# Second attention of a fused transformer block: turned weights in two 64-row tiles, values and projections in every second step

## The chip, the core and the metric

The kernel runs on one core of one Trainium2 chip, as one launch. Its time is device microseconds (us) from start to end, the median of three runs: 1046.44 us (1045.92 to 1047.82). The core has a matrix engine (TensorE, PE in the profile, with its weight loads shown apart as PEld), VectorE (DVE), ScalarE (ACT), GpSimd (POOL), and SyncE (SP), which issues DMAs. PSUM is what PE writes its results to, in eight banks.

## The reference

Six residual parts follow each other on x, 8 sequences of 256 tokens by 128 channels, in float32. The change touches only the fifth:

```
x = x + 0.5 * _L0_ffn_ref(_layernorm(x), ...)      # stage f0
x = x + _L0_attn_ref(_layernorm(x), ...)           # a0
x = x + 0.5 * _L0_ffn_ref(_layernorm(x), ...)      # g0
x = x + 0.5 * _L1_ffn_ref(_layernorm(x), ...)      # f1
x = x + _L1_attn_ref(_layernorm(x), ...)           # a1: what is changed
x = x + 0.5 * _L1_ffn_ref(_layernorm(x), ...)      # g1

def _attn_forward(X, Wq, bq, Wk, Wv, Wproj, bproj, Wr, br, b_nd):   # 16 heads of 64
    Q = X @ Wq + bq;  K = X @ Wk;  V = X @ Wv
    R = X @ Wr + br                                # 10 numbers a head and token
    extra = einsum('bhtn,ntp->bhtp', R, D_ntT)     # a learned bias by distance
    logits = Q @ K^T / 8 + causal mask + extra
    A = softmax(logits) @ V
    return A @ Wproj + bproj
```

## The kernel before, in words

Stage a1 is `attention_one`. It goes through 8 batches of 8 steps: 64 steps n, each for one pair of heads of one batch b, with u = n mod 8 the step within the batch. Every engine has its own program, in order; semaphores tie them.

For a pair (two heads, 256 queries by 256 keys; the causal half is left out, so 3 blocks of 128x128 a head):

- `scores` (PE, L2655): Q times K^T into PSUM banks 0 and 1, one head each, from the 64 rows 0 to 63 and the 64 rows 64 to 127 of the array. A float32 product is two instructions in the profile, so x8.
- `logits` (DVE, L2839 and L2841): adds the bias and takes the row's least value. Two heads a step. `scores` of the next step waits for both (`l_ready`).
- `probabilities` (ACT, L2781 and L2783): exp and row sums, two heads.
- `invert` and `normalise` (DVE, L2849, L2585, L2586): divides by the sums.
- `turn` (PE, L2667): in step n for pair n - 1, six 128x128 transposes, head i into bank 2 + i. It waits for the normalised weights (`pn_ready`) and for the bank (`pT_ready`).
- `take_turned` (ACT, L2791): two copies of 128x384, PSUM to PT.
- `values` (PE, L2687): in step n for pair n - 3, weights times V into bank 4, each head in its own 64 columns of the array.
- `take_values` (ACT, L2799): a 128x256 copy of bank 4 to AT (the profile calls it a_xn).
- `project` (PE, L2700, once a batch at u = 3): A times Wproj, 32 instructions, then `add` on DVE (L2858).

Between these PE makes pieces for a later batch, each one PSUM bank: Q, K, V and R projections in three parts of reduced precision (L743 to L745), and G, the bias tables, by `tables` (L2611, two 40-row matmuls side by side a pair of pieces). STEPS and `pair_pieces` say which step makes which piece: before, one Q in every even step and its K in the next odd step, V in steps u = 5, 6, 7, R at u = 0, and a G pair at u = 1 to 4. `pieces_stored` copies them out of PSUM, odd numbers mostly by ACT, even ones by DVE, after the step's logits (DVE) or exps (ACT). Three banks are used in turn for pieces.

Within a step PE's order is: scores, tables, values, projections, (project), turn. DVE's is: logits, pieces, invert and normalise. ACT's is: take_turned of pair n - 2, exps, pieces, take_values.

Of the kernel before, what the change touches and what calls it, by code (L numbers as in the profile page):

```python
# [19 lines left out]
ACT = mybir.ActivationFunctionType  # L20
# [3 lines left out]
P = 128  # L24
BATCH = 8
# [2368 lines left out]
def attention_one(core, name, ctx, w):  # L2394
# [26 lines left out]
    def chunk(b, c):  # L2421
# [4 lines left out]
    SLOTS = 4  # L2426

    VLAG = 3
    TSLOTS = 2 * VLAG
    L = sb("L", [P, SLOTS, 3 * P])  # L2430
    least = sb("least", [P, SLOTS, 2])
# [25 lines left out]

    STEPS = ([("R", 0), ("QK", 0)], [("G", 0), ("G", 1), ("QK", 1)], [("G", 2), ("G", 3), ("QK", 2)],  # L2460
             [("G", 4), ("G", 5), ("QK", 3)], [("G", 6), ("G", 7), ("QK", 4)],
             [("QK", 5), ("V", 0)], [("QK", 6), ("V", 1), ("V", 2)], [("QK", 7), ("V", 3)])
# [4 lines left out]
    def pair_pieces(n):  # L2467

        found = []
        for b in range(2, BATCH, 2):  # L2470
            for j in range(CH):
                first = CH * b + 2 * j - QK_AHEAD
                for which, at in (("Q", first), ("K", first + (j < CH - 1))):
                    if at == n:
                        found.append((b, (which, j)))
        return found

    def in_step(n):

        b, u = n // CH, n % CH  # L2480
        own = [(b + 1, k) for k in STEPS[u] if k[0] != "QK" or b == 0] if b + 1 < BATCH else []
        return ([k for k in own if k[1][0] in "RG"] + pair_pieces(n) + [k for k in own if k[1][0] not in "RG"]
                + ([(b - 1, ("O", 0))] if u == VLAG and b else []))
# [104 lines left out]
    def tensor(pe):  # L2588
# [68 lines left out]
                        last.then_inc(s_done, 1)  # L2657

        def turn(b, c):
            for i in range(2):  # L2660
                n = b * H1 + 2 * c + i
                pe.wait_ge(pn_ready, n + 1)
                if n >= 2:

                    pe.wait_ge(pT_ready, n - 1)
                for j in range(3):
                    last = pe.transpose(bank[2 + i][:, P * j:P * j + P], pr[:, n % SLOTS, P * j:P * j + P],  # L2667
                                        core.ident[:, :])
                last.then_inc(p_turned, 1)

        def values(b, c):
            s, m = b % 2, b * CH + c
            pe.wait_ge(pT_ready, 2 * m + 2)
            if c == 0:
                for j in range(4):
                    wait_piece(pe, b, "V", j)
            if m:

                pe.wait_ge(aT_ready, m)
# [3 lines left out]
            o = bank[4]  # L2683
            for kt, keys, queries in ((0, slice(0, SEQ), slice(0, SEQ)), (1, slice(SEQ, 3 * P), slice(P, SEQ))):
                for i in range(2):
                    h = 2 * c + i
                    last = pe.matmul(o[D1 * i:D1 * i + D1, queries], V[s][:, kt, D1 * h:D1 * h + D1],  # L2687
                                     PT[:, (2 * m + i) % TSLOTS, keys], start=(kt == 0), stop=(kt == 1),
                                     skip_group_check=True)
            last.then_inc(pv_done, 1)  # L2690

        def project(b):

            pe.wait_ge(aT_ready, CH * (b + 1))
# [14 lines left out]
        for n in range(BATCH * CH + VLAG):  # L2709
            b, u = n // CH, n % CH  # L2710
            if b < BATCH:
                scores(b, u)
            if b + 1 < BATCH:
                tables(n)
            if 0 <= n - VLAG:
                values((n - VLAG) // CH, (n - VLAG) % CH)
            if b < BATCH:
                projections(n)
            if u == VLAG and b:
# [50 lines left out]
    def scalar(act):  # L2770
        act.wait_ge(core.const_ready, 4)
        act.activation(ln.unused[:, 0:1], core.ones[:, 0:1], ACT.Exp)
        ln.take_quarter(act, 0)

        def probabilities(n):
            o = n % SLOTS
            act.wait_ge(l_ready, n + 1)
            if n >= SLOTS:

                act.wait_ge(p_turned, n - SLOTS + 1)  # L2780
# [5 lines left out]
        def take_turned(n):  # L2786
            act.wait_ge(p_turned, n + 1)
            if n >= TSLOTS:

                act.wait_ge(pv_done, (n - TSLOTS) // 2 + 1)  # L2790
            act.activation(PT[:, n % TSLOTS, :], bank[2 + n % 2][:, 0:3 * P], ACT.Copy).then_inc(pT_ready, 1)  # L2791

        def take_values(m):
            b, c = m // CH, m % CH
            act.wait_ge(pv_done, m + 1)
            if b:

                act.wait_ge(piece_done, at(b - 1, ("O", 0))[0] + 1)
            act.activation(AT[:, c, :], bank[4][:, 0:SEQ], ACT.Copy).then_inc(aT_ready, 1)  # L2799

        for n, k in enumerate(FIRST):
            if by_act(k):
                store_piece(act, True, 0, k)
            if n in (6, 10, 14):
                ln.take_quarter(act, (6, 10, 14).index(n) + 1)
        for n in range(BATCH * CH + VLAG):
            b, u = n // CH, n % CH
            if 2 <= n < BATCH * CH + 2:
                for i in range(2):
                    take_turned(2 * (n - 2) + i)  # L2810
# [5 lines left out]
            if 0 <= n - VLAG:  # L2816
                take_values(n - VLAG)

    def vector(dve):
        ln.statistics_of(dve, 0, 4)  # L2820
# [42 lines left out]
                store_piece(dve, False, 0, k)  # L2863
        for n in range(BATCH * CH):
            b, u = n // CH, n % CH
            if u == VLAG + 1 and b:
                add(b - 1)
            for i in range(2):
                logits(b, 2 * u + i)
# [144 lines left out]
```

## Time and profile before

| | us |
|---|---|
| median of three runs | 1046.44 |
| profiled execution, span from first to last instruction | 1041.4 |
| stage a1, first scores to the last add | 615.72 to 904.10 |
| PE, DVE, ACT busy over the span | 893.2, 759.6, 524.4 |

The profiled execution's span is 5.0 us less than the median time; what lies outside the span is not in the trace. In a list of instructions the first number is the start in us from the span's start, the second how long the group took. Matmuls overlap: one may start while the one before still drains, so the distance between starts tells what a matmul costs, not its own duration.

### The profile page before, as it was taken

The page shows a single profiled execution, that of the slowest core. Times are in us where ns is not written, and L with a number is a line of the kernel's source. Part 1 is how long each engine was busy: PE and PEld are TensorE (multiplying, and loading weights), DVE is VectorE, ACT ScalarE, POOL GpSimd, SP SyncE. Part 2 cuts the span into 40 slices and gives each one's busy share as a digit, 9 for nine tenths or more (in the row PEclk, how much of TensorE's full clock was granted, in tenths as well). Part 3 has the DMA queues.
Part 4 walks back from the last instruction along what each step waited for, and adds up shares of the span by engine and source line. Part 5 has one row for each costly group of instructions (what it writes and reads, how often), then busy time and mean ns, then how long its engine had stood idle before and what let it go on. Part 6 is the DMA issues. An engine that isn't in the chain of part 4 may idle for free.

```text
span 1041.4 us, 22929 instructions
## 1 busy us (share of the span) xinstructions
PE 893.2 (86%) x7108; PEld 676.9 (65%) x7108; DVE 759.6 (73%) x2654; ACT 524.4 (50%) x1461; POOL 287.2 (28%) x395
## 2 busy tenths in 40 slices
PE   5899979999996899945999199999999999649992
PEld 4467756666765357834999167777777776437992
DVE  7758888787767866877676757787678777566675
ACT  4232044555564323023455258787778778534553
POOL 3034046543001003127755260001000000067751
PEclk9999996998997999965999589999999999958997
DMA  9204089800005204065320266435634642153413
GB/s 233 69 2 137 1 312 374 257 5 1 3 1 159 77 1 138 1 189 164 90 73 29 81 205 201 142 105 160 197 101 130 182 143 61 58 166 84 109 35 125
DMA packets 134948, 119.73 MB, mean 115 GB/s; under 512 B 10755, under 2 KB 115227, under 8 KB 134836
## 3 DMA queue, kind: packets, MB, share of 16 engines
q1 hardware_dynamic: 130292, 109.83, 35.5%
q0 software_dynamic: 4544, 8.54, 2.5%
q8 instruction: 55, 0.90, 0.4%
q14 instruction: 57, 0.47, 0.1%
HBM read 67.45 MB, written 51.80 MB: 115 GB/s over the span
## 4 chain that ended last, share of the span: by engine, by line
PE 75%; DVE 14%; issue 4%; ACT 3%; DMA 2%; DVEq 1%; SPq 0%; POOL 0%; POOLq 0%; ACTq 0%
PE psum L955 7%; PE psum L964 7%; PE psum L1551 6%; PE psum L1465 4%; PE psum L2655 4%; PE psum L2687 4%; PE psum L743 3%; PE psum L2667 3%; PE psum L2139 3%; PE psum L2611 3%; PE psum L2700 3%; PE psum L2077 3%; PE psum L745 2%; PE psum L744 2%; PE psum L2042 2%
## 5 line engine op out<-in xcount | busy, mean ns | idle before, releaser
L2297 DVE TENSOR_REDUCE a_negmax<-psum 128x2 f32<-128x512 f32 x128 | 83.9, 684 | 24.2 <-PE psum L2077 22.8
L2246 ACT ACTIVATE a_PT<-psum 128x1024 f32<-128x1024 f32 x64 | 65.5, 1023 | 28.0 <-PE psum L2122 27.6
L2781 ACT ACTIVATE a_pr<-a_L,a_least 128x128 f32<-128x128 f32 x128 | 50.8, 397 | 38.5 <-DVE a_least L2841 38.1
L2687 PEld LDWEIGHTS psum<-a_PT,a_V 128*64 128x64 f32 x512 | 32.8, 136 | 47.6 <-issue 24.1
L2783 ACT ACTIVATE a_pr<-a_L,a_least 128x256 f32<-128x256 f32 x128 | 63.6, 497 | 0.0
L1010 ACT ACTIVATE f_hT<-psum,f_wt 128x128 f32<-128x128 f32 x156 | 44.5, 369 | 36.2 <-PE psum L955 36.2
L2687 PE MATMUL psum<-a_PT,a_V 128*64 128x256 f32 (+1 forms) x512 | 55.7, 337 | 7.0 <-ACT a_xn L2799 6.9
L1010 ACT ACTIVATE g_hT<-psum,g_wt 128x128 f32<-128x128 f32 x156 | 44.5, 369 | 33.5 <-PE psum L955 33.5
L2655 PE MATMUL psum<-a_KT,a_Q 64*128 64x128 f32 (+1 forms) x512 | 59.3, 350 | 0.3 <-DVE a_least L2841 0.3
L2791 ACT ACTIVATE a_PT<-psum 128x384 f32<-128x384 f32 x128 | 55.4, 488 | 0.7 <-PE psum L2667 0.6
L2116 PE MATMUL psum<-a_turned 24*128 24x256 f32 x256 | 55.4, 366 | 0.0
L2841 DVE CUSTOM_DVE_ANT_0 a_L<-psum,a_X 128x256 f32<-128x256 f32 x128 | 53.7, 419 | 0.0
L2077 PE MATMUL psum<-a_turned 24*128 24x256 f32 x224 | 52.5, 346 | 0.9 <-ACT a_turned L2212 0.7
L2667 PE MATMUL psum<-ident,a_pr 128*128 128x128 f32 x384 | 52.8, 274 | 0.0
L163 POOL MEMSET g_logit<- 128x128 f32 x1 | 0.2, 205 | 180.4 <-DVEq L2916 180.4
L2667 PEld LDWEIGHTS psum<-ident,a_pr 128*128 128x128 f32 x384 | 44.9, 141 | 7.5 <-issue 1.4
L2122 PE MATMUL psum<-a_shift,ahead_select 32*128 32x256 bf16 x256 | 48.4, 294 | 0.0
L896 POOL DMA_INDIRECT f_back_dram<-f_y,f_xin x39 | 41.3, 1059 | 25.6 <-DVE f_y L1093 22.0
L896 POOL DMA_INDIRECT g_back_dram<-g_y,g_xin x39 | 40.9, 1048 | 25.0 <-DVE g_y L1093 21.3
L2839 DVE CUSTOM_DVE_ANT_0 a_L<-psum,a_X 128x128 f32<-128x128 f32 x128 | 36.7, 286 | 14.6 <-PE psum L2655 14.3
L955 PE MATMUL psum<-f_xT,f_wt 128*128 128x128 f32 x312 | 43.2, 284 | 3.1 <-DVE f_xT L1087 3.1
L2586 DVE TENSOR_SCALAR a_pr<-a_pr,a_rinv 128x256 f32<-128x256 f32 x128 | 45.5, 355 | 0.0
(579 smaller groups left out, 2593.7 us busy)
## 6 DMA issues: line engine op xcount, KB each, us to landing
z<-a_G SPq DMA_DIRECT2D x32, 512.0 KB, 3.4
a_X<-z SPq DMA_DIRECT2D x16, 1024.0 KB, 6.8
f_slots_dram<-empty SPq DMA_DIRECT2D x1, 8910.0 KB, 28.1
g_slots_dram<-empty SPq DMA_DIRECT2D x1, 8910.0 KB, 51.3
a_X<-z SPq DMA_DIRECT2D x16, 512.0 KB, 4.0
f_wgu<-in_gate_up SPq DMA_DIRECT2D x16, 384.0 KB, 6.9
z<-pad SPq DMA_DIRECT2D x6, 1024.0 KB, 9.8
g_wgu<-in_gate_up SPq DMA_DIRECT2D x16, 384.0 KB, 6.3
```

Of the source, the lines that this page charges most:

```text
L896: pool.indirect_dma_start(back_dram[:, :], bass.IndirectOffsetOnAxis(ap=xin[:, i, P:P + 1].bitcast(I32), axis=0), y[i % YBUF][:, :], None, ...
L955: last = pe.matmul(bank[i % 2][:, P * c:P * c + P], wt[i % WBUF][:, P * c:P * c + P], xT[:, i % 2, :], start=True, stop=True)
L964: last = pe.matmul(bank[4 + i % 2][:, 0:P], hT[:, i % 2, c, :], wt[i % WBUF][:, OUT + P * c:OUT + P * c + P], start=(c == 0), stop=(c == F ...
L1010: act.activation(hT[:, i % 2, c, :], bank[i % 2][:, P * c:P * c + P], ACT.Relu, bias=wt[i % WBUF][:, B1 + c:B1 + c + 1]).then_inc(relu_don ...
L1551: last = pe.matmul(sum_bank[g], ypart[:, p, i, :].bitcast(F32R), ST[:, p % RING, BLOCK * g:BLOCK * g + BLOCK].bitcast(F32R), start=(p == 0 ...
L2077: last = pe.matmul(bank[h % 2][:, SEQ * t:SEQ * t + SEQ], q[rows, g, P * t:P * t + P].bitcast(F32R), k[rows, g, :].bitcast(F32R), start=Tr ...
L2246: act.activation(PT[m % 4][:, :, :, :].rearrange("p j t n -> p j (t n)"), core.psum[:, 2 + 2 * (u % 2):4 + 2 * (u % 2), :], ACT.Exp, scale ...
L2297: dve.tensor_reduce(negmax[:, :, h], query_bank(b, h).rearrange("p (t n) -> p t n", n=SEQ), AX.X, ALU.max, negate=True).then_inc(max_done, 1)
L2655: last = pe.matmul(out, Q[rows, at, b % 2, queries], KT[rows, at, b % 2, keys], start=True, stop=True)
L2667: last = pe.transpose(bank[2 + i][:, P * j:P * j + P], pr[:, n % SLOTS, P * j:P * j + P], core.ident[:, :])
L2687: last = pe.matmul(o[D1 * i:D1 * i + D1, queries], V[s][:, kt, D1 * h:D1 * h + D1], PT[:, (2 * m + i) % TSLOTS, keys], start=(kt == 0), st ...
L2783: act.activation(pr[:, o, P:3 * P], L[:, o, P:3 * P], ACT.Exp, bias=least[:, o, 1:2], scale=-1.0, accum_out=sums[:, o, 1:2]).then_inc(p_re ...
```

## The change

1. `turn` splits every 128x128 transpose into two, from rows 0 to 63 and rows 64 to 127 of the weights: 12 transposes of 64 rows, each moving 64 columns. Rows 0 to 63 of both heads go to bank 2, rows 64 to 127 to bank 3. It waits once for the copy of the whole pair before (`pT_ready`, m).
2. `take_turned` is one ACT copy for a pair, 768 elements a partition out of two banks.
3. `values` runs only in even steps, for pairs n - 4 and n - 3, into the two halves of bank 4. `take_values` is one 128x512 copy for both.
4. All Q, K, V and R pieces are made in even steps; G pairs in odd steps (but for one in step 2 of the first batch). R and the first G pair of a batch are made two batches ahead, at u = 6 and 7. `project` moves from u = 3 to u = 4.

```diff
+    STEPS = ([("QK", 0), ("QK", 1)], [("G", 2), ("G", 3)], [("QK", 2), ("QK", 3), ("V", 0)], [("G", 4), ("G", 5)],
+             [("QK", 4), ("QK", 5), ("V", 1)], [("G", 6), ("G", 7)], [("QK", 6), ("QK", 7), ("V", 2), ("V", 3)], [])
+    SECOND = {0: [("R", 0)], 1: [("G", 0), ("G", 1)], 2: [("G", 2), ("G", 3)]}
+    FIRST_GATES = {6: [("R", 0)], 7: [("G", 0), ("G", 1)]}
...
-                first = CH * b + 2 * j - QK_AHEAD
-                for which, at in (("Q", first), ("K", first + (j < CH - 1))):
-                    if at == n:
-                        found.append((b, (which, j)))
+                if CH * b + 2 * j - QK_AHEAD == n:
+                    found += [(b, ("Q", j)), (b, ("K", j))]
...
         def turn(b, c):
+            m = b * CH + c
+            if m:
+                pe.wait_ge(pT_ready, m)
             for i in range(2):
...
-                if n >= 2:
-                    pe.wait_ge(pT_ready, n - 1)
                 for j in range(3):
-                    last = pe.transpose(bank[2 + i][:, P * j:P * j + P], pr[:, n % SLOTS, P * j:P * j + P],
-                                        core.ident[:, :])
-                last.then_inc(p_turned, 1)
+                    for r in range(2):
+                        rows = slice(HP * r, HP * r + HP)
+                        at = HP * (3 * i + j)
+                        last = pe.transpose(bank[2 + r][:, at:at + HP], pr[rows, n % SLOTS, P * j:P * j + P],
+                                            core.ident[rows, rows])
+            last.then_inc(p_turned, 1)
...
-            if 0 <= n - VLAG:
-                values((n - VLAG) // CH, (n - VLAG) % CH)
+            if n % 2 == 0 and n >= VSTEP:
+                for m in (n - VSTEP, n - VLAG):
+                    values(m // CH, m % CH)
...
-            act.activation(PT[:, n % TSLOTS, :], bank[2 + n % 2][:, 0:3 * P], ACT.Copy).then_inc(pT_ready, 1)
+            own = PT[:, 2 * (m % VLAG):2 * (m % VLAG) + 2, :].rearrange("p i n -> p (i n)")
+            act.activation(own.rearrange("p (k r c) -> p r k c", r=2, c=HP),
+                           core.psum[:, 2:4, 0:3 * P].rearrange("p r (k c) -> p r k c", c=HP),
+                           ACT.Copy).then_inc(pT_ready, 1)
...
-            act.activation(AT[:, c, :], bank[4][:, 0:SEQ], ACT.Copy).then_inc(aT_ready, 1)
+            act.activation(AT[:, c:c + 2, :].rearrange("p c n -> p (c n)"), bank[4], ACT.Copy).then_inc(aT_ready, 1)
```

How PE's order changes in the steady part of the stage. Before, one whole step (u = 1 of a later batch); L2655 is scores, L2611 tables, L2687 values, L743 to L745 the K piece, L2667 turn:

```order
L2655 MATMUL psum<-a_KT,a_Q 128x128 x2
L2655 MATMUL psum<-a_KT,a_Q 128x256 x2
L2611 MATMUL psum<-early_bnd,a_RT 128x512 x2
L2687 MATMUL psum<-a_PT,a_V 64x256 x2
L2687 MATMUL psum<-a_PT,a_V 64x128 x2
L743 MATMUL psum<-a_xs_high,early_wk_rest 128x512
L744 MATMUL psum<-a_xs_rest,early_wk_high 128x512
L745 MATMUL psum<-a_xs_high,early_wk_high 128x512
L2667 MATMUL psum<-ident,a_pr 128x128 x6
```

Now, from a K piece at the end of the even step u = 0 through the odd step u = 1; L2683 is turn, L2667 scores, L2623 tables:

```order
L743 MATMUL psum<-a_xs_high,early_wk_rest 128x512
L744 MATMUL psum<-a_xs_rest,early_wk_high 128x512
L745 MATMUL psum<-a_xs_high,early_wk_high 128x512
L2683 MATMUL psum<-ident,a_pr 128x64 x12
L2667 MATMUL psum<-a_KT,a_Q 128x128 x2
L2667 MATMUL psum<-a_KT,a_Q 128x256 x2
L2623 MATMUL psum<-early_bnd,a_RT 128x512 x2
L2683 MATMUL psum<-ident,a_pr 128x64 x12
```

Values and the K piece have left the odd step; what stays in it, and the turn before it, use 64 or 40 rows of the array and all 128 columns.

ACT, before, at the end of such a step (exps, pieces, values copy, the two turned copies, the next exps):

```order
L2781 ACTIVATE a_pr,a_sums<-a_L,a_least 128x128
L2783 ACTIVATE a_pr,a_sums<-a_L,a_least 128x256
L2731 ACTIVATE a_G<-psum 128x512
L2731 ACTIVATE a_KT<-psum 128x512
L2799 ACTIVATE a_xn<-psum 128x256
L2791 ACTIVATE a_PT<-psum 128x384 x2
```

Now, at the end of the even step u = 0:

```order
L2798 ACTIVATE a_pr,a_sums<-a_L,a_least 128x128
L2800 ACTIVATE a_pr,a_sums<-a_L,a_least 128x256
L2748 ACTIVATE a_KT<-psum 128x512
L2819 ACTIVATE a_xn<-psum 128x512
L2809 ACTIVATE a_PT<-psum 128x2x6x64
```

The G piece has moved to the odd step, the values copy is twice as wide and comes every second step, and the turned copy is one instruction, still behind all of these.

## Rows read from the trace of the kernel before

**Rows 1.** The page: busy time of the engines

```profile
PE 893.2 (86%) x7108; PEld 676.9 (65%) x7108; DVE 759.6 (73%) x2654; ACT 524.4 (50%) x1461; POOL 287.2 (28%) x395
```

**Rows 2.** Stretches: from:to, length, busy of engines; batches 0, 1-5, 6, 7

```profile
615.72:649.39 33.67, 31.91 (x236) 22.46 (x235) 27.78 (x130) 26.73 (x97) 2.26 (x5) 1.00 0.70 205
649.39:830.96 181.57, 181.09 (x1331) 129.78 (x1330) 137.94 (x623) 140.52 (x491) 5.38 (x8) 1.00 0.50 146
830.96:865.79 34.83, 34.83 (x261) 24.87 (x260) 26.43 (x123) 27.00 (x96) 0.00 (x0) 1.00 0.51 152
865.79:904.10 38.31, 31.14 (x271) 23.40 (x270) 22.49 (x119) 28.52 (x102) 0.00 (x0) 1.00 0.01 2
```

**Rows 3.** PE instructions in order of time: start, took, instruction

```profile
790.79 0.93 PE L2655 MATMUL psum<-a_KT,a_Q 64*128 64x128 f32 x8
791.65 0.87 PE L2687 MATMUL psum<-a_PT,a_V 128*64 128x256 f32 x8
792.45 0.50 PE L743 MATMUL psum<-a_xs_high,early_wk_rest 128*128 128x512 f32 x1
792.79 0.39 PE L744 MATMUL psum<-a_xs_rest,early_wk_high 128*128 128x512 f32 x1
793.02 0.40 PE L745 MATMUL psum<-a_xs_high,early_wk_high 128*128 128x512 f32 x1
...
797.89 0.82 PE L2667 MATMUL psum<-ident,a_pr 128*128 128x128 f32 x6
798.64 0.93 PE L2655 MATMUL psum<-a_KT,a_Q 64*128 64x128 f32 x8
799.39 1.03 PE L2611 MATMUL psum<-early_bnd,a_RT 40*128 40x512 f32 x4
```

**Rows 4.** The chain, same columns: a G pair and a project

```profile
843.96 0.86 PE psum L2611 x4
846.51 3.57 PE psum L2700 x32
```

**Rows 5.** PE instructions elsewhere, at half clock (last row: that stretch's clock)

```profile
332.00 1.81 PE L1393 MATMUL psum<-g_wr,g_xnT 128*128 128x64 f32 x8
333.60 1.06 PE L632 MATMUL psum<-ident,g_xn 128*128 128x128 f32 x4
334.45 3.52 PE L1393 MATMUL psum<-g_wr,g_xnT 128*128 128x64 f32 x16
...
329.40:337.90 8.50, 8.50 (x43) 8.50 (x43) 7.98 (x40) 5.26 (x11) 0.00 (x0) 0.50 1.05 291
```

**Rows 6.** Step 40: its scores, and the first and last row of its logits

```profile
794.69 0.93 PE L2655 MATMUL psum<-a_KT,a_Q 64*128 64x128 f32 x8
...
795.64 0.29 DVE L2839 CUSTOM_DVE_ANT_0 a_L<-psum,a_X 128x128 f32<-128x128 f32 x1 [0.15 <-PE psum L2655]
796.76 0.08 DVE L2841 DVE_READ_ACCUMULATOR2_ANT a_least<- 128x1 f32 x1
```

**Rows 7.** DVE and ACT in the last batch, where PE is not full

```profile
885.99 0.28 DVE L2839 CUSTOM_DVE_ANT_0 a_L<-psum,a_X 128x128 f32<-128x128 f32 x1
886.66 0.40 ACT L2781 ACTIVATE a_pr<-a_L,a_least 128x128 f32<-128x128 f32 x1 [0.35 <-DVE a_least L2841]
888.43 0.36 ACT L2799 ACTIVATE a_xn<-psum 128x256 f32<-128x256 f32 x1
889.22 0.28 DVE L2839 CUSTOM_DVE_ANT_0 a_L<-psum,a_X 128x128 f32<-128x128 f32 x1
```

**Rows 8.** ACT groups by shape: mean ns of one after the busy time

```profile
L2791 ACT ACTIVATE a_PT<-psum 128x384 f32<-128x384 f32 x80 | 34.6, 489 | 0.0
L2731 ACT ACTIVATE a_G<-psum 128x512 f32<-128x512 f32 x20 | 11.6, 580 | 0.0
L2246 ACT ACTIVATE a_PT<-psum 128x1024 f32<-128x1024 f32 x64 | 65.5, 1023 | 28.0 <-PE psum L2122 27.6
```

**Rows 9.** DVE group: a G piece copied out of PSUM

```profile
L2744 DVE COPY a_G<-psum 128x512 f32<-128x512 f32 x20 | 13.7, 686 | 0.0
```

More of the change, by code:

```diff
@@ L2428, in attention_one @@
     VLAG = 3
+    VSTEP = 4
+    HP = P // 2
     TSLOTS = 2 * VLAG
@@ L2471, in pair_pieces, with gates_in_step @@
             for j in range(CH):
-                first = CH * b + 2 * j - QK_AHEAD
-                for which, at in (("Q", first), ("K", first + (j < CH - 1))):
-                    if at == n:
-                        found.append((b, (which, j)))
-        return found
+                if CH * b + 2 * j - QK_AHEAD == n:
+                    found += [(b, ("Q", j)), (b, ("K", j))]
+        return found
+    def gates_in_step(n):
+        b, u = n // CH, n % CH
+        own = []
+        if b == 0:
+            own += [(1, k) for k in SECOND.get(u, [])]
+        if b + 1 < BATCH:
+            own += [(b + 1, k) for k in STEPS[u] if k[0] == "G" and not (b == 0 and u == 1)]
+        if b + 2 < BATCH:
+            own += [(b + 2, k) for k in FIRST_GATES.get(u, [])]
+        return own
     def in_step(n):
         b, u = n // CH, n % CH
-        own = [(b + 1, k) for k in STEPS[u] if k[0] != "QK" or b == 0] if b + 1 < BATCH else []
-        return ([k for k in own if k[1][0] in "RG"] + pair_pieces(n) + [k for k in own if k[1][0] not in "RG"]
-                + ([(b - 1, ("O", 0))] if u == VLAG and b else []))
+        own = [(b + 1, k) for k in STEPS[u] if k[0] == "V" or (k[0] == "QK" and b == 0)] if b + 1 < BATCH else []
+        return gates_in_step(n) + pair_pieces(n) + own + ([(b - 1, ("O", 0))] if u == VSTEP and b else [])
     pieces, in_bank = {}, [0] * len(PIECE_BANKS)
@@ L2676, in values @@
                     wait_piece(pe, b, "V", j)
-            if m:
-                pe.wait_ge(aT_ready, m)
+            if m >= 2:
+                pe.wait_ge(aT_ready, m // 2)
             else:
@@ L2682, in values @@
                 pe.wait_ge(piece_read[i], first_reads[i])
-            o = bank[4]
+            o = bank[4][:, SEQ * (m % 2):SEQ * (m % 2) + SEQ]
             for kt, keys, queries in ((0, slice(0, SEQ), slice(0, SEQ)), (1, slice(SEQ, 3 * P), slice(P, SEQ))):
@@ L2692, in project @@
         def project(b):
-            pe.wait_ge(aT_ready, CH * (b + 1))
+            pe.wait_ge(aT_ready, CH // 2 * (b + 1))
             _, i, used = at(b, ("O", 0))
@@ L2712, in tensor @@
                 scores(b, u)
-            if b + 1 < BATCH:
+            if b < BATCH:
                 tables(n)
-            if 0 <= n - VLAG:
-                values((n - VLAG) // CH, (n - VLAG) % CH)
+            if n % 2 == 0 and n >= VSTEP:
+                for m in (n - VSTEP, n - VLAG):
+                    values(m // CH, m % CH)
             if b < BATCH:
                 projections(n)
-            if u == VLAG and b:
+            if u == VSTEP and b < BATCH and b:
                 project(b - 1)
@@ L2778, in probabilities @@
             if n >= SLOTS:
-                act.wait_ge(p_turned, n - SLOTS + 1)
+                act.wait_ge(p_turned, (n - SLOTS) // 2 + 1)
             act.activation(pr[:, o, 0:P], L[:, o, 0:P], ACT.Exp, bias=least[:, o, 0:1], scale=-1.0,
@@ L2808, in scalar @@
             if 2 <= n < BATCH * CH + 2:
-                for i in range(2):
-                    take_turned(2 * (n - 2) + i)
+                take_turned(n - 2)
             if b < BATCH:
@@ L2815, in scalar @@
                 pieces_stored(act, True, n)
-            if 0 <= n - VLAG:
-                take_values(n - VLAG)
+            if n % 2 == 0 and n >= VSTEP:
+                take_values(n - VSTEP)
     def vector(dve):
@@ L2865, in vector @@
             b, u = n // CH, n % CH
-            if u == VLAG + 1 and b:
+            if u == VSTEP + 1 and b:
                 add(b - 1)
```

17 lines of the change are left out of this document (7 added, 10 removed).

## The prediction

> **What bounds the kernel now.** I read the page first: PE is busy 86% of the span, DVE 73%, ACT 50% [rows 1]. The reader is to see from it only which engine to follow; what the change is worth is decided in stage a1. So I cut that stage by its batches in the view by windows. In batches 1 to 5 PE is busy 181.09 of 181.57 us, that is 36.31 us a batch without a gap, while DVE and ACT are busy 137.94 and 140.52, some 76%. Batch 6 is full too (34.83 of 34.83). In batch 7, which makes no pieces, PE is busy 31.14 of 38.31 [rows 2]. PE binds 56 steps of 64; the last 8 hang on something else, which the order of time shows: from one pair's logits to the next are 889.22 - 885.99 = 3.23 us, logits, exps, inversion and logits again. The change leaves that loop alone [rows 7].
>
> A PE that is "busy" is not at work all the time, and here the view in order of time matters most. A float32 matmul column costs 0.86 / 1024 = 0.84 ns: a G pair is two instructions of 512 columns on either of two row groups, together 0.86 us [rows 4]. Scores, values and transposes all stream 768 such columns a step (scores and values side by side in two tiles), 0.65 us each. The starts say more than that: transposes to scores 0.75, scores to tables 0.75, scores to values 0.86, values to the K piece 0.80, and in that piece 0.34 to the second part against 0.23 to the third [rows 3]. The surplus sits only where the shape that the array is used in changes (128 rows, 64 rows, 64 columns): transposes to scores 0.10 before and 0.10 after, scores to values 0.11, values to pieces 0.15 on both sides of the values, and 0.11 in the piece's first part. No surplus lies between scores (64 rows) and tables (40 rows). That is 0.57 us for the three changes of shape that each step has.
>
> Check: a batch of before is 8 x (3 x 0.65 + 0.57) = 20.2, 4 Q and 4 K pieces at 3 x 0.23 = 0.69, so 5.5, four V 2.8, R 0.7 (its columns are those of a Q piece), four G pairs 3.4, project 3.57 [rows 4]: 36.1, measured 36.31. The 0.2 is short waits, and I add it to the new sum too.
>
> **The change part by part.**
> Order of work on PE: even steps keep three changes of shape (scores to values to pieces to turn); odd steps are scores, tables, turn, all of 64 or 40 rows, and have none. In the 28 step pairs of batches 0 to 6 that is 28 x 0.57 = 16.0 us less on PE. All else on PE keeps its amount; the second `values` of a pair follows the first in the same shape.
>
> Transposes: 12 of 64 columns in two row groups, for 6 of 128. Where the granted clock was 0.50 (1.2 GHz) the trace has both sizes with 128x128 float32 weights: transposes of 128 columns start (334.45 - 333.60) / 4 = 0.21 us apart, and matmuls of only 64 columns (333.60 - 332.00) / 8 = 0.20 apart [rows 5]. Half the columns bought nothing; the weights, 128 columns in both, set the pace. In `turn` the weights stay 128 columns wide, so each row group needs 0.65 us for its six, as now. The two groups should overlap, as they do for scores, whose eight instructions take the time of four [rows 3]. Bounds: 0.32 us a step if only moved columns counted, 1.29 if the groups did not overlap; I take 0.65, no gain, since that is what both nearest rows give.
> The Trainium skill has rules on both sides. TensorEngine Tiling (Array Packing), section Theoretical Speedup, gives a contraction of at most 64 up to twice the speed; TensorE: Matmul & The Clock Gate, section LDWEIGHTS, says a load costs by its columns and not by its rows. By the first a turn would take 0.32 us, by the second 0.65; the rows at 1.2 GHz agree with the second.
>
> ACT: one 768-wide copy for two of 384 (489 ns each). Between 512 (580) and 1024 (1023) a straight line gives 0.80 us, about 0.70 before the next may start, against two overlapped ones at about 0.8 [rows 8]; bounds 0.49 (one of them alone) and 1.02. Values copy: one of 0.58 [rows 8] for two of 0.36 [rows 7]. ACT gets some 0.2 us a pair of steps back, which nobody waits for.
>
> What is late next: an odd step now holds 0.65 + 0.86 + 0.65 = 2.16 us of PE work, less than others need.
> (a) The next scores wait for both heads' logits. Scores to logits start is 0.95, logits last 1.20 [rows 6]; with 0.1 to hand over, 2.25: at least 0.1 is lost in each odd step.
> (b) Pair u = 0, 1, from the scores of step 0: these waited for the logits of the step before, so its exps (0.89 a head, from (888.43 - 886.66) / 2 [rows 7]) end at 1.3, DVE's inversion of head 1 (0.65) at 2.0, logits of step 0 at 3.2, its exps at 4.5, ACT's K copy (0.5) at 5.0, values copy at 5.5, the turned copy only then, at 6.3. Turn in step 1 waits for it; behind turn stand the scores of step 2, at 6.96. PE's own sum is 4.54 + 2.16 = 6.70.
> (c) Pair 2, 3: DVE's order puts the V piece before the inversion. PE hands V over at 4.5; copy (686 ns long, 0.6 until the next [rows 9]), two inversions and two logits (0.6 + 1.3 + 1.2) end at 7.7; scores at 7.76, PE's sum 5.23 + 2.16 = 7.39.
> (d) Pair 4, 5: 8.80 with V and project, then 2.25: 11.05 for 10.96. Project holds ACT's values copy too, but the turned copy fits in the odd step.
> (e) Pair 6, 7: 6.61 with R and two V, 0.15 for a bank that V waits for, 2.25: 9.0 for 8.77.
> Sum 34.8 for a PE sum of 33.8, so 1.0 of 2.3 us is handed back; with the 0.2 of waits 35.0 against 36.31, 1.3 less a batch.
>
> Over the stage: batches 1 to 5, 5 x 1.3 = 6.5. Batch 0 makes R and the first G pair of batch 2 on top, 0.69 + 0.86, which eats its own 1.5: 0. Batch 6 has given its R and G pair away and its last pair is without Q, K: 2 x 6.96 + 7.76 + 11.05 = 32.8, + 0.2, against 34.83: 1.8. Batch 7 is the 3.23 us loop: an even step there has 3.2 us of PE work, hidden by it. The tail's copy is 0.2 longer (0.58 for 0.36), as the last two pairs' values share it: +0.2. SP's transfers of bias tables start up to one step later for heads 8 to 15 and are needed about seven steps on, and the 35.0 us batch still covers them; the cost if not would be a wait of DVE, none now.
> Total: -6.5 - 1.8 + 0.2 = -8.1. The span of the profiled execution falls from 1041.4 to 1033.3; the median of before, 1046.44, is 5.0 above that span, so 1038.3 us.
>
> **Rivals.**
> A, the forecast: -8.1. Its own range is -13 to -4, from 0.15 us more or less in each of 28 odd steps.
> B, slower: the row groups' transposes do not overlap. Every turn costs 0.64 more. For it: no row here shows a transpose in a half of the rows. Against it: scores and G pairs do overlap, in float32. Price: 56 x 0.64 = 36 on a bound PE, less the 16.0 saved; the odd steps then have no slack to hand back: +20, 1066. It turns slower once a turn costs over 0.15 us more than now.
> C, transposes faster: only moved columns count, 0.32 saved. Odd steps cannot use it, even ones do: 28 x 0.32 = 9 more, 1029. The same time nearly results if the odd steps hand nothing back (-16, 1030). Against C: rows 5.
> D, the odd steps hand all back: each needs 0.6 us more than PE's 2.16, not 0.25. For it: DVE and ACT need 3.23 us a pair by themselves [rows 7], 6.46 in two, and a piece or two on top, near the 6.70 of PE; a copy out of two banks that is slower than a line through the widths of rows 8 adds in (b) straight to the path. Against it: most pieces fit in DVE's wait for exps. Time: 1046, -2 to +2.
> Beside them, the clock after the stage: a stage that ends 8 us earlier meets the changes of the granted clock in the stage behind it at other points of the work; at 1.2 GHz a transpose takes 0.21 us for 0.11 [rows 5, 3], an estimated 2 us either way.
>
> **How the numbers follow.** A 0.62, C 0.15, D 0.13, B 0.10. About 2 us, 0.2%, is what a measurement tells from no change. Faster takes A, C and a quarter of D: 0.80. Same takes half of D: 0.07. Slower: B and the last quarter of D: 0.13. The range 1030 to 1045 holds A, half of C and of D.
>
> **What would show it.** PE's rows after: twelve transposes that start two and two together, 0.107 us from two to two (B: one by one; C: 0.053). No surplus between an odd step's scores, tables and turn. Odd steps of 2.25 to 2.5 us from scores to scores; PE idle before scores (on DVE's logits) and before turn (on ACT's turned copy), together 1 us a batch. A turned copy of 0.8 us. Batches 1 to 5 at 35.0 us, batch 7 at 38. I am wrong if a turn takes other than 0.65 to 0.75, or if odd steps are over 2.7 us, or if the surplus at a change of shape grows where values come in twos.

## The result, and the profile after

The changed kernel takes 1029.77 us (median of 4 runs, 1024.85 to 1031.29); the kernel before, run beside it, 1046.18. The ratio is 0.9857, 95% interval 0.9819 to 0.9895: 15.0 us faster by the ratio (16.4 between the medians), where 8.1 was forecast. The sign and the stage were right, the size was short by nearly half, and 1029.77 lies 0.2 us below the range. A second set of runs of the same kernel gave 1031.15 and a ratio of 0.9864 (0.9824 to 0.9904). Two of the twelve runs of experiment 2 below, its profiled one among them, fell in a slower state of the chip, so its time and ratio are of the other ten.

The page and the view by windows of the changed kernel, to be read against [rows 1, 2]. The windows run from the first scores of a batch to those of the next; columns: from:to, length, then busy time and instructions of PE, PEld, DVE, ACT and POOL, granted clock (1 is full), share of the DMA engines, GB/s.

```profile
span 1028.6 us, 23449 instructions
PE 869.1 (84%) x7492; PEld 662.6 (64%) x7492; DVE 760.1 (74%) x2654; ACT 518.8 (50%) x1365; POOL 286.6 (28%) x395
```

```profile
616.71:650.32 33.61, 29.80 (x280) 21.82 (x279) 28.52 (x127) 25.83 (x84) 3.76 (x6) 1.00 0.64 187
650.32:821.70 171.38, 164.85 (x1571) 120.62 (x1571) 138.06 (x626) 137.67 (x431) 3.87 (x6) 1.00 0.52 153
821.70:853.71 32.01, 30.02 (x299) 21.91 (x299) 25.55 (x122) 26.65 (x86) 0.00 (x0) 1.00 0.49 145
853.71:891.24 37.53, 30.06 (x338) 22.42 (x334) 22.66 (x120) 27.64 (x87) 0.00 (x0) 0.95 0.14 42
```

The reader is to see three things. Batch 0 stayed at 33.6 us, batches 1 to 5 went from 181.57 to 171.38, batch 6 from 34.83 to 32.01, batch 7 from 38.31 to 37.53. Together the stage is 13.8 us shorter, from 288.4 to 274.5 (from the first scores to the last add). The stage starts 1.0 later, what lies behind it is the same 137.4, and 1041.4 - 13.8 + 1.0 = 1028.6, the span. Second, PE is no longer full: 164.85 busy of 171.38, 6.5 us idle where 0.5 was. Third, DVE does what it did (138.06 for 137.94), and ACT 2.9 us less (137.67 for 140.52).

The medians differ by 2 to 4 us more than the two spans, and that is scatter from outside the stage. Each run's time is 1.7 to 1.9 us above its own span, so most of the 5.0 between span and median of before came of a profiled execution that was quicker than the median. In the traces of all kernels here the stage, behind the same code, starts between 611.3 us (mean granted clock so far 0.90, experiment 3) and 620.8 us (0.88, both orders of experiment 5).

PE in order of time, from a K piece through a whole odd step (start, us, instruction), to be held against [rows 3]:

```profile
791.17 0.40 PE L745 MATMUL psum<-a_xs_high,early_wk_high 128*128 128x512 f32 x1
791.49 0.59 PE L2683 MATMUL psum<-ident,a_pr 64*128 64x64 f32 x12
791.92 0.87 PE L2667 MATMUL psum<-a_KT,a_Q 64*128 64x128 f32 x8
792.63 1.02 PE L2623 MATMUL psum<-early_bnd,a_RT 40*128 40x512 f32 x4
793.73 0.59 PE L2683 MATMUL psum<-ident,a_pr 64*128 64x64 f32 x12
```

From the turn's start at 791.49 to the scores' start are 0.43 us, against 0.75 before. The single starts in the trace are two and two together (2 to 4 ns), the second pair 0.11 behind the first and the others 0.061 to 0.064 from pair to pair; before, six starts were 0.109 apart. So 0.32 us went here: 0.10 of a change of shape, and 0.22 of the transposes themselves. That 0.10 is not saved behind a K piece: it now lies ahead of the turn (0.32 from the piece's last part, where 0.23 lies inside a piece). Scores to tables are 0.71, tables to turn 0.86 where PE did not wait (799.95 to 800.82 further on). The turn at 793.73 waited for ACT's copy:

```profile
791.93 0.57 ACT L2748 ACTIVATE a_KT<-psum 128x512 f32<-128x512 f32 x1
792.41 0.57 ACT L2819 ACTIVATE a_xn<-psum 128x512 f32<-128x512 f32 x1
792.89 0.79 ACT L2809 ACTIVATE a_PT<-psum 128x768 f32<-128x768 f32 x1
```

The largest waits of PE and of its weight loads for another engine in batches 1 to 5 (engine, what, waited for: us in total, times, longest). PEld runs ahead of PE, so what it waits is not all lost to PE:

```profile
PEld psum L2683 <- ACT a_PT L2809: 10.5, 20, 0.9
PE psum L2667 <- DVE a_least L2860: 6.2, 11, 0.8
```

The eight steps of batch 5, from scores to scores: before 3.95 4.06 4.07 7.63 4.08 3.90 4.70 3.90 (36.3); after 4.32 2.31 5.02 2.94 8.59 2.26 6.41 2.25 (34.1). The even steps are what PE's starts add up to without a wait. For an odd step they add up to 0.71 + 0.86 + 0.43 = 2.00; what is above 2.00 is waiting, 1.76 us in this batch.

### The profile page after: what moved, and what is told of

Same layout as the page of the kernel before. It is cut to its first block, busy times and chain, and to the rows that moved or that the text cites. A ratio compares the mean times of both kernels' runs of the same rounds, so it can differ in the third digit from the quotient of the medians.

```text
span 1028.6 us, 23449 instructions
## 1 busy us (share of the span) xinstructions
PE 869.1 (84%) x7492; PEld 662.6 (64%) x7492; DVE 760.1 (74%) x2654; ACT 518.8 (50%) x1365; POOL 286.6 (28%) x395
## 4 chain that ended last, share of the span: by engine, by line
PE 65%; DVE 20%; ACT 6%; issue 6%; DMA 2%; DVEq 1%; SPq 0%; POOL 0%; ACTq 0%; POOLq 0%
PE psum L955 7%; PE psum L964 7%; PE psum L1551 6%; PE psum L1465 5%; PE psum L2139 3%; PE psum L2703 3%; PE psum L2716 3%; PE psum L2077 3%; PE psum L2667 2%; PE psum L743 2%; DVE a_negmax L2297 2%; PE psum L1491 2%; PE psum L2042 2%; ACT a_pr L2800 2%; PE psum L745 2%
## 5 line engine op out<-in xcount | busy, mean ns | idle before, releaser
L2667 PE MATMUL psum<-a_KT,a_Q 64*128 64x128 f32 (+1 forms) x512 | 58.5, 346 | 11.1 <-DVE a_least L2860 10.3
L1010 ACT ACTIVATE g_hT<-psum,g_wt 128x128 f32<-128x128 f32 x156 | 44.3, 368 | 33.6 <-PE psum L955 33.6
L2683 PEld LDWEIGHTS psum<-ident,a_pr 64*128 64x128 f32 x768 | 30.6, 139 | 34.6 <-ACT a_PT L2809 21.5
L2809 ACT ACTIVATE a_PT<-psum 128x768 f32<-128x768 f32 x64 | 51.1, 798 | 1.2 <-PE psum L2683 1.2
L2703 PE MATMUL psum<-a_PT,a_V 128*64 128x256 f32 (+1 forms) x512 | 49.5, 335 | 0.1
L955 PE MATMUL psum<-g_xT,g_wt 128*128 128x128 f32 x312 | 42.7, 281 | 2.2 <-DVE g_xT L1087 2.2
L2667 PEld LDWEIGHTS psum<-a_KT,a_Q 64*128 64x128 f32 x512 | 35.1, 190 | 14.1 <-issue 13.8
```

The costliest lines, as they stand in the source:

```text
L955: last = pe.matmul(bank[i % 2][:, P * c:P * c + P], wt[i % WBUF][:, P * c:P * c + P], xT[:, i % 2, :], start=True, stop=True)
L1010: act.activation(hT[:, i % 2, c, :], bank[i % 2][:, P * c:P * c + P], ACT.Relu, bias=wt[i % WBUF][:, B1 + c:B1 + c + 1]).then_inc(relu_don ...
L2667: last = pe.matmul(out, Q[rows, at, b % 2, queries], KT[rows, at, b % 2, keys], start=True, stop=True)
```

## The experiments

The measure that tells kernels apart below is the length of batches 1 to 5 in a profiled execution: the change itself gave 171.38 and, unchanged in a later set, 171.46, while whole times scatter by several us.

**1. The order alone.** The new order, with the turns and their copy as one instruction of 128 rows and contiguous columns.

```diff
                 for j in range(3):
-                    for r in range(2): ...
+                    last = pe.transpose(bank[2 + i][:, P * j:P * j + P], pr[:, n % SLOTS, P * j:P * j + P],
+                                        core.ident[:, :])
```

> The new order of pieces and values, but turn as six 128x128 transposes again (one ACT copy a pair stays). Theory S (a change of the array's shape costs 0.15 to 0.2 us, and a tiled turn 0.43 us against 0.65): the odd step gets two changes back (tables to turn, turn to scores), so a pair of steps has 5 changes, where the changed kernel has 3 and the kernel before 6. PE's odd step is 0.65 + 0.86 + 0.65 + 0.4 = 2.56 us, over the 2.25 that scores and logits need, so it binds again: pairs 0.2 us shorter than before, some 5 us in all, 1040 to 1043. Rival O (the gain is the order itself, values in twos and fewer waits, whatever the shape of turn): 1030 to 1034.

Measured: 1039.77, ratio 0.9966 (0.9942 to 0.9989).

```profile
646.80:824.87 178.07, 177.15 (x1331) 129.65 (x1331) 138.99 (x626) 139.59 (x432) 3.87 (x6) 1.00 0.49 145
```

3.5 us less than 181.57, with PE nearly full (177.15 of 178.07), and a time just under the 1040 to 1043 expected. A turn of 128 rows keeps a change of shape ahead of and behind it, so a pair of steps has five changes for six. The one that goes is values to pieces, 0.25 us in [rows 3] (0.80 for 0.65 behind the values, 0.34 for 0.23 in the piece), 5 us in 20 pairs. Not all of it stays: an odd step needs 2.46 us by PE's starts, and took 2.52 to 2.91.

**2. The tiles alone.** The order of before; `turn`, its wait and its copy as changed.

```diff
+            m = b * CH + c
+            if m:
+                pe.wait_ge(pT_ready, m)
...
-                    last = pe.transpose(bank[2 + i][:, P * j:P * j + P], pr[:, n % SLOTS, P * j:P * j + P], ...
+                    for r in range(2): ...
```

> The order of before, with turn in tiles and one ACT copy a pair. Theory S: three changes of shape a step as before, turn 0.43 for 0.65: 0.2 us in each of 56 steps that PE fills, 11 us less, 1033 to 1037. Rival (tiles are worth nothing but for the change of shape they save, my forecast's 0.65 for a turn): 1044 to 1047.

Measured: 1040.54, ratio 0.9959 (0.9926 to 0.9993), where 1033 to 1037 was expected.

```profile
652.49:830.39 177.90, 171.62 (x1576) 116.56 (x1574) 137.09 (x624) 138.43 (x451) 5.45 (x9) 1.00 0.51 150
```

```profile
798.24 0.39 PE L745 MATMUL psum<-a_xs_high,early_wq_high 128*128 128x512 f32 x1
798.57 0.59 PE L2671 MATMUL psum<-ident,a_pr 64*128 64x64 f32 x12
798.99 0.87 PE L2656 MATMUL psum<-a_KT,a_Q 64*128 64x128 f32 x8
```

The turn takes 0.42 here too, so its saving belongs to the tiles and not to the order. The change of shape has moved from behind the turn to ahead of it (piece to turn 0.33, against 0.23 inside a piece): still six a pair. A step without a wait is 0.28 shorter (u = 1: 3.78 for 4.06), so 40 steps were to give 11 us. 3.7 went, and PE is idle 6.3 us, most of it before `values`, which wait for ACT's copy of bank 4:

```profile
PE psum L2691 <- ACT a_xn L2805: 5.1, 10, 0.7
```

Order alone -3.5, tiles alone -3.7, both -10.2. Both together take the changes of shape out of the odd step, which neither does alone, and the new order has half as many copies of bank 4 to wait for; no run parts these two.

**3. Twelve plain products.** `turn` as changed, in float32 matmuls with the identity instead of transposes.

```diff
-                        last = pe.transpose(bank[2 + r][:, at:at + HP], pr[rows, n % SLOTS, P * j:P * j + P],
-                                            core.ident[rows, rows])
+                        last = pe.matmul(bank[2 + r][:, at:at + HP], pr[rows, n % SLOTS, P * j:P * j + P],
+                                         core.ident[rows, rows], start=True, stop=True)
```

> The changed kernel with the same twelve tiles turned as plain float32 products with the identity instead of transposes: two instructions each, same weights of 64x128, same 64 moved columns. Theory W (a float32 product's weight load of 128 columns takes 0.107 us and sets the pace, a transpose's takes half): 12 pairs of starts 0.107 apart, turn 1.29 us, time 1055 to 1066. Rival M (moved columns set the pace in both): 0.054 to 0.063 apart, turn 0.65 to 0.75, time 1034 to 1040.

Measured: 1060.08 (one run), within the 1055 to 1066 of theory W.

```profile
647.89:845.02 197.13, 197.13 (x2054) 158.15 (x2054) 139.33 (x626) 142.84 (x432) 3.86 (x6) 1.00 0.45 134
```

```profile
801.35 1.55 PE L2683 MATMUL psum<-ident,a_pr 64*128 64x64 f32 x24
802.74 0.88 PE L2667 MATMUL psum<-a_KT,a_Q 64*128 64x128 f32 x8
```

The same shapes (weights of 64 x 128, 64 moved columns), but 24 instructions for 12, and the pairs 0.112 apart instead of 0.062: turn to scores 1.39 us, against 0.43. The products of `project`, which move 128 columns, are 0.112 apart as well (3.57 / 32 [rows 4]), so for products half the moved columns buy nothing, as I had read from [rows 5]. The weight loads differ in the same sense. PEld by line and shape: count, busy us, mean ns of one, idle before. First the changed kernel, then this one:

```profile
L2667 PEld LDWEIGHTS psum<-a_KT,a_Q 64*128 64x128 f32 x321 | 21.9, 188 | 8.7 <-issue 8.6
L2703 PEld LDWEIGHTS psum<-a_PT,a_V 128*64 128x64 f32 x320 | 19.8, 137 | 12.4 <-issue 6.6
L2683 PEld LDWEIGHTS psum<-ident,a_pr 64*128 64x128 f32 x480 | 19.1, 138 | 19.2 <-ACT a_PT L2809 10.5 <-issue 8.0
```

```profile
L2683 PEld LDWEIGHTS psum<-ident,a_pr 64*128 64x128 f32 x912 | 55.4, 188 | 14.7 <-issue 9.6 <-ACT a_PT L2809 4.5
```

A load of 128 columns lasts 188 ns for a product and 138 for a transpose, as long as a product's load of 64 columns (137). That the loads set the pace in both cases is argued from this and not shown. The trace of before had this sign, and the prediction did not use it (the same view, turn and scores):

```profile
L2667 PEld LDWEIGHTS psum<-ident,a_pr 128*128 128x128 f32 x242 | 28.8, 141 | 4.8
L2655 PEld LDWEIGHTS psum<-a_KT,a_Q 64*128 64x128 f32 x322 | 21.1, 186 | 6.8 <-issue 6.5 <-ACT a_Q L2755 0.2 <-DVE x L2858 0.2
```

**4. Values apart.** The second `values` of a pair behind the pieces, on the same work. What was expected counts two more changes of shape in each even step. It is one: pieces to values and values to turn are new, but pieces to turn is gone. Only at u = 4, where `project` stands between values and turn, are there two.

```diff
-                for m in (n - VSTEP, n - VLAG):
-                    values(m // CH, m % CH)
+                values((n - VSTEP) // CH, (n - VSTEP) % CH)
             if b < BATCH:
                 projections(n)
+            if n % 2 == 0 and n >= VSTEP:
+                values((n - VLAG) // CH, (n - VLAG) % CH)
```

> The changed kernel, but the second values of an even step stand behind the projections: no work more or less, two more changes of shape in each of 28 even steps. Theory S: 0.15 to 0.2 us for the first (pieces to values) and the same for the second (values to turn, as values to pieces before): 0.35 x 28 = 10 us more than the changed kernel, 1038 to 1042. Rival (the surplus at a change of shape is a wait on data that would be elsewhere without it): 1029 to 1033.

Measured: 1034.71, ratio 0.9914 (0.9883 to 0.9945).

```profile
652.80:826.73 173.93, 170.83 (x1570) 119.38 (x1571) 138.76 (x626) 138.81 (x431) 3.73 (x6) 1.00 0.51 152
```

```profile
794.87 0.40 PE L745 MATMUL psum<-a_xs_high,early_wk_high 128*128 128x512 f32 x1
795.20 0.87 PE L2703 MATMUL psum<-a_PT,a_V 128*64 128x256 f32 x8
796.00 0.58 PE L2683 MATMUL psum<-ident,a_pr 64*128 64x64 f32 x12
```

The steps by themselves give the price: u = 0 went from 4.32 to 4.47 and u = 2 from 5.02 to 5.17, 0.15 for one change, without a wait in either; u = 4 went from 8.59 to 8.94, 0.35 for two. At u = 6 (6.41 to 7.18) only 0.15 of the 0.77 is shape. The rest is in the last two pieces, both V: PE now reaches them before their banks are free. In batch 5 they start 0.31 and 0.57 us behind the part before, where 0.23 is usual, and each begins at the slow pace of a first part. The second of them:

```profile
822.36 0.50 PE L743 MATMUL psum<-early_wv_high,a_xs_rest 128*128 128x512 f32 x1 [0.17 <-ACT a_Q L2773]
```

Together the 20 even steps grew from 121.7 to 128.8, of which 5 x (3 x 0.15 + 0.35) = 4.0 is shape. The odd steps shrank from 49.7 to 45.1, which is 20 times 2.25, since DVE and ACT caught up meanwhile. So even steps that are 7.1 us longer cost 2.55. This is the hand-back seen from the other side: here nearly two thirds of what the even steps lost was slack in the odd ones. The time, 1034.71, is under the 1038 to 1042 expected, for the change too many and for this.

**5. Which queue makes the odd step wait.** Four kernels that only move copies in ACT's or DVE's order. ACT: the values copy goes from the end of an even step to the odd step, behind the turned copy. DVE: V pieces are stored behind the inversions instead of ahead. Both together. And all of DVE's pieces in even steps behind the inversions, on top of ACT's (`not n % 2` for `k[0] == "V"`).

```diff
 ACT     take_turned(n - 2)
+        if n % 2 and n > VSTEP:
+            take_values(n - 1 - VSTEP)
...
-        if n % 2 == 0 and n >= VSTEP:
-            take_values(n - VSTEP)
+        take_values(BATCH * CH - 2)
 DVE
-            pieces_stored(dve, False, n)
+            own = [(s, k) for s, k in in_step(n) if k[0] != "O" and not by_act(k)]
+            for s, k in own:
+                if k[0] != "V":
+                    store_piece(dve, False, s, k)
             for i in range(2):
                 invert(b, 2 * u + i)
+            for s, k in own:
+                if k[0] == "V":
+                    store_piece(dve, False, s, k)
```

> The changed kernel; on ACT the values copy now stands behind the next turned copy instead of ahead of it. If what holds the odd step is ACT's queue ahead of the turned copy (my account b), turn comes 0.5 us sooner in pair 0, 1: 0.3 us a batch and more, stage a1 272 or less against 274.5. If DVE's logits end last there anyway (they end 0.1 us before the scores of step 42 in the changed kernel's trace), nothing much is won: 274 to 275.

> The changed kernel; on DVE the V pieces are copied after the step's inversions instead of ahead of them. If V's late arrival from PE holds inversion, next logits and next scores (my account c), step u = 3 falls from 2.94 us to 2.3 to 2.6 and a batch by 0.3 to 0.6: stage a1 271 to 273. If DVE is simply full in that pair, the copy costs the same behind: 274 to 275.

> Both reorderings. If each frees its own wait they add: stage a1 270 to 272, time 3 us under the changed kernel. If they wait for the same thing, no better than the better of the two.

> As both reorderings, but every piece that DVE copies in an even step (Q, K, R too) stands behind the inversions. If the handed back time in odd steps is the inversion waiting behind late pieces, odd steps come to 2.25 us all: stage a1 268 to 270. Against it, PE's next pieces wait for these banks, three in turn: then even steps get longer by up to 0.5 us and the stage is 276 or more.

Measured: ACT's order 1034.38, 0.9906 (0.9875 to 0.9937); DVE's order 1029.19, 0.9856 (0.9828 to 0.9885); both 1032.35, 0.9874 (0.9851 to 0.9897), with 170.35 for batches 1 to 5; all pieces late 1055.83 (one run). The windows of the first, second and fourth:

```profile
647.93:819.29 171.36, 164.23 (x1570) 121.55 (x1571) 138.06 (x626) 138.53 (x431) 3.86 (x6) 1.00 0.50 150
```

```profile
647.33:817.69 170.36, 164.82 (x1570) 120.24 (x1572) 136.98 (x626) 137.80 (x431) 3.86 (x6) 1.00 0.52 155
```

```profile
652.57:841.48 188.91, 167.42 (x1571) 120.18 (x1571) 138.71 (x626) 139.07 (x431) 3.77 (x6) 1.00 0.46 137
```

And in the fourth, PE in order of time:

```profile
749.58 3.81 PE L2716 MATMUL psum<-early_wp,a_xn 128*128 128x128 f32 x32 [1.36 <-DVE a_Q L2774]
```

ACT's order is worth nothing in batches 1 to 5 (171.36 for 171.38), though the turn no longer waits for it there (tables to turn is 0.86 in all 20 odd steps, and was up to 1.11): the next scores wait for DVE's logits all the same. Its time of 1034.38 has another part: in its profiled execution batch 7 is 4 us longer, with 10.2 us at a lower clock (below). The kernel with both orders has a longer batch 7 too (40.0), so the order may bring this about; no run shows whether it does.

DVE's order is worth 1.0 in batches 1 to 5 and 1.5 in batch 0 (32.05 for 33.61), and loses 0.4 in batch 6. The stage came to the 271 to 273 us expected (272.3), but not by the way expected: step u = 3 fell to 2.85 only, not to 2.3 to 2.6. Of the 1.0, half is step u = 3 and half is step u = 7, and this second half comes from batch 2 alone, where an odd step of 3.13 us fell to 2.46; more on that step at the end. The whole time (ratio 0.9856) does not tell this kernel from the changed one (0.9857 and 0.9864). Both orders together give in batches 1 to 5 what DVE's gives alone, so the two gains do not add. Holding back Q, K and R as well costs 17.5: PE then waits for their banks.

**6. A piece into the fullest odd step's slack.** Step u = 3 is the longest odd step (2.94), with 1 us of wait. One V piece goes there from u = 2; in a second kernel DVE's order is changed as well.

```diff
-    STEPS = (..., [("QK", 2), ("QK", 3), ("V", 0)], [("G", 4), ("G", 5)],
+    STEPS = (..., [("QK", 2), ("QK", 3)], [("G", 4), ("G", 5), ("V", 0)],
```

> The changed kernel, but the first V piece of a batch is made in the odd step u = 3, between tables and turn, instead of in u = 2. PE gets two changes of shape more there (0.2 each). If step u = 3 (2.94 us for 1.94 of PE work) is held by DVE, which still copies a V piece and inverts, its slack takes the piece: even step u = 2 is 0.69 shorter (5.02 to 4.33), u = 3 is 1.94 + 0.69 + 0.4 = 3.0, a batch 0.5 to 0.6 less, stage a1 271 to 272. If V is late for DVE there instead, u = 3 grows to 3.5 and nothing is won.

> The same, and V copied by DVE behind the inversions as in e7: that copy can then not hold the step's inversions while PE makes V. Stage a1 269 to 271, time 4 to 5 us under the changed kernel. If DVE is merely full in those two steps, as e10.

> The changed kernel as it is, for runs on the same chip as e10 and e11: ratio to before 0.983 to 0.990. The clock's low stretches before and behind the stage move its time by some 5 us from run to run; stage a1 itself 274 to 275 where its clock stays at 2.4 GHz, and up to 4 us more where it falls in the last batch.

Measured: piece moved 1028.72, 0.9852 (0.9814 to 0.9889); with DVE's order 1024.38, 0.9805 (0.9767 to 0.9842); the changed kernel again 1031.15. Windows, in that order:

```profile
649.62:818.45 168.83, 166.26 (x1571) 118.85 (x1571) 137.32 (x626) 137.75 (x431) 3.87 (x6) 1.00 0.52 154
```

```profile
649.67:817.85 168.18, 166.38 (x1570) 118.64 (x1572) 136.92 (x626) 137.84 (x431) 3.79 (x6) 1.00 0.53 155
```

```profile
651.42:822.88 171.46, 164.93 (x1571) 120.64 (x1571) 138.07 (x626) 137.69 (x431) 3.87 (x6) 1.00 0.52 153
```

Steps u = 2 and 3 go from 5.02 + 2.94 to 4.33 + 3.17: the even step loses the whole piece, 0.7, the odd one gets 0.23 longer for it. PE's idle time falls from 6.5 to 2.6 and 1.8 us. The second kernel is the fastest of all, 6.8 us below the changed one run beside it; 5.5 of that is the stage, 269.1 for 274.6 in the profiled executions.

Not tried: transposes of 64 columns from weights of all 128 rows, which would part the effect of the moved columns from that of the two row groups.

## Why the prediction was right and wrong

**PE binds, and the three changes of shape of the odd step go: right.** They are gone from the rows of an odd step. Their price was a little too high: scores to tables still take 0.71 where no change of shape lies ahead, so only 0.05 of the 0.10 that I gave to that place is a change. Three are worth 0.50 us, not 0.57. Experiment 4 shows the same from the other side, 0.15 for one and 0.35 for two, without other work. The copies came as forecast too: the turned copy 798 ns for 0.80, and one values copy of 0.58.

**The turn: wrong, and this is the step that failed:** "Half the columns bought nothing; the weights, 128 columns in both, set the pace." The rule was read from a product ([rows 5], L1393) and applied to a transpose. Experiment 3 shows that it holds for products (0.112 apart with 64 moved columns and with 128) and the changed kernel that it does not hold for transposes (0.062), whose loads are shorter by a quarter. A turn takes 0.43, not 0.65: 0.22 less, 8 x 0.22 = 1.8 a batch. That is the direction of rival C (0.15), with 0.22 for its 0.32; that C's 1029 is also the measured time is in part luck, since the stage fell by 13.8 and not by its 17. Whether the moved columns or the split into row groups made the turn short is open. Rival B, no overlap, is refuted by starts two and two together. Of the Trainium skill's two rules, the first, TensorEngine Tiling (Array Packing), Theoretical Speedup (up to twice with a contraction of at most 64), comes nearer to the transposes here, 0.65 to 0.43; the second, TensorE: Matmul & The Clock Gate, LDWEIGHTS, says that rows do not count, which the transposes bear out (141 ns with 128 rows, 138 with 64); that the columns count holds for the products (188 ns for 128, 137 for 64), but columns alone do not give the time, since a transpose's load of 128 was no longer than a product's of 64.

**The hand-back: right in kind, too small in size.** With turns of 0.43 and three changes at 0.50, PE's sum is 36.1 - 4 x 0.50 - 8 x 0.22 = 32.3 us a batch. Batches 1 to 5 took 34.28 each, so 1.9 came back as waits, all of it in odd steps; I had 1.0, and 0.2 for short waits in other places that did not come. Most of the difference is the same 0.22 again: an odd step has 2.00 us of PE work, not 2.16, but still cannot end before 2.25. Three of the four odd steps took 2.25 to 2.31, as (a) had it. C's remark that odd steps cannot use a faster turn was right as well.

Pair by pair (before the 0.2 for short waits), forecast and measured in batch 5: 6.96 and 6.63; 7.76 and 7.96; 11.05 and 10.85; 9.0 and 8.66. Three pairs gained from the turn. (b) named ACT's queue for the first; experiment 5 shows that moving ACT's copy changes nothing, so that account is wrong as a cause, although the turn's wait for ACT is in the rows. The wait report names the last to come; behind it DVE's logits came just as late (their last row ends at 794.07, 0.15 before the scores, the distance that it also has in step u = 3). (c) has the one pair that took longer. The last part of PE's V piece and DVE in that stretch, start and us:

```profile
798.49 0.40 PE L745 MATMUL psum<-early_wv_high,a_xs_high 128*128 128x512 f32 x1
798.23 0.69 DVE L2776 COPY a_KT<-psum 128x512 f32<-128x512 f32 x1 [0.91 <-PE psum L745]
798.92 0.69 DVE L2779 COPY a_V<-psum 128x512 f32<-128x512 f32 x1
799.53 0.15 DVE L2868 RECIPROCAL a_rinv<-a_sums 128x2 f32<-128x2 f32 x1
...
801.61 0.42 DVE L2860 CUSTOM_DVE_ANT_0 a_L<-psum,a_X 128x256 f32<-128x256 f32 x1
801.95 0.08 DVE L2860 DVE_READ_ACCUMULATOR2_ANT a_least<- 128x1 f32 x1
```

DVE works from 798.23 to 802.03 without a gap: the K copy, the V copy, two inversions, two logits; scores follow at 802.18. My sum (c) had V handed over 4.5 us behind the scores of step 2 (here at 794.22); the copy starts at 4.70, where the last product of V ends (798.49 + 0.40), and that is the 0.2. The K copy, which I left out, ends just then, so in this order it costs nothing. With V behind the inversions it is the K copy that starts the row, and the step moved only from 2.94 to 2.85: DVE is full from there whatever the order. What helped was less before the step (experiment 6).

**Rival D, all handed back (0.13): refuted in full, half true.** Of 18.8 us that the odd steps' shapes (10.0) and the turns (8.8) free in batches 1 to 5, 10.2 stayed.

**Batches 0, 6, 7.** Batch 0: nothing gained, as said, though for more than its added work: DVE's order alone got 1.5 there. Batch 6: -2.8 for -1.8, in the main the turns again. Batch 7: -0.8 for +0.2; no run explains it.

**The sum.** -6.5 - 1.8 + 0.2 became -10.19 - 2.82 - 0.78 (batch 7) - 0.06 (batch 0) = -13.85. The term that was mis-sized is the turn, 0.43 for 0.65. A batch came to 34.3 and not 35.0: 1.8 more saved by the turns, 0.3 less by the shapes, 0.9 more handed back, and the 0.2 of short waits not needed. Over batches 1 to 5 that is 3.7 of the 5.7 missing; batches 6 and 7 have 1.0 each.

## What to carry to other kernels

Take the price of an instruction from rows of the same operation: in float32 here, the weight loads of a transpose and of a product of the same shape lasted 138 and 188 ns, and the view of the weight loads shows such a difference beforehand. Count changes of shape on both sides of an edit, and read their price from single steps that have no wait: the sum over 20 steps in experiment 4 fitted a wrong count by accident (0.355 a step, as if for two changes). When the bound engine gets faster in alternate steps, work out for each short step when the other engines can be through; that floor (here 2.25 us, scores to logits to scores) decides what the saving is worth, and the slack in it can be filled with a piece from a long step. A report names the wait that came last, not the one that would remain: only moving the named copy showed that it was not the cause.

## What the runs showed that was not expected

**The clock in the last batch.** PE has less work there than before (30.06 busy for 31.14), and the granted clock fell to half (1.2 GHz) for 3.4 us in the changed kernel. A window over it:

```profile
859.70:863.10 3.40, 3.33 (x28) 2.15 (x24) 2.70 (x17) 2.72 (x10) 0.00 (x0) 0.50 0.00 0
```

PE in order of time: it had waited 1.50 us for ACT just before, and scores that take 0.87 took 1.65.

```profile
859.44 0.74 PE L2683 MATMUL psum<-ident,a_pr 64*128 64x64 f32 x12 [1.50 <-ACT a_PT L2809]
860.24 1.65 PE L2667 MATMUL psum<-a_KT,a_Q 64*128 64x128 f32 x8
```

Batch 7 took 37.5 us with this stretch and also without one (DVE's order), 41.5 with 10.2 us at half clock (ACT's order), 41.8 with as much in experiment 2. Up to 4 us of a whole time go with it; since these kernels differ in their order too, how much of that is the clock's is not parted.

**DVE beside GpSimd.** Twice in the stage (step u = 7 of batches 0 and 2) an odd step took 3.1 instead of 2.25 us. In one, two GpSimd operations and a DVE normalisation (usually 0.36) lie side by side, and the latter took 0.83 and ended 0.15 us after the second GpSimd operation:

```profile
716.44 0.84 POOL L734 TENSOR_TENSOR a_xs_rest<-a_xnT,a_xs_high 128x256 fp32r<-128x256 f32 x1
717.25 0.72 POOL L2567 TENSOR_TENSOR x<-x,early_bp_row 128x256 f32<-128x256 f32 x1
717.29 0.83 DVE L2598 TENSOR_SCALAR a_pr<-a_pr,a_rinv 128x256 f32<-128x256 f32 x1
719.38 0.93 PE L2667 MATMUL psum<-a_KT,a_Q 64*128 64x128 f32 x8 [0.80 <-DVE a_least L2860]
```

With DVE's order of experiment 5 the same two GpSimd operations in batch 0 fall beside the V copy and the logits, which read PSUM, and these keep their lengths:

```profile
644.75 0.68 DVE L2779 COPY a_V<-psum 128x512 f32<-128x512 f32 x1
645.27 0.73 POOL L734 TENSOR_TENSOR a_xs_rest<-a_xnT,a_xs_high 128x256 fp32r<-128x256 f32 x1
646.21 0.42 DVE L2860 CUSTOM_DVE_ANT_0 a_L<-psum,a_X 128x256 f32<-128x256 f32 x1
```

That step took 2.25 us, where it was 3.14. So the work on GpSimd costs here only where it meets a normalisation, and this is where most of what DVE's order gained lies: 0.9 of the 1.5 us of batch 0, and half of the 1.0 of batches 1 to 5. The rows show which operations suffer side by side; why they do is argued, since no experiment took the GpSimd work away. The Trainium skill has a rule that would give it, Advanced Engine Details and Errata, VectorE Performance Modes: the second port of VectorE to SBUF is shared with GpSimd. No row shows which ports an operation used.
